# A pipelined six-layer local-attention kernel: the layer loop written out as 96 steps, and four changes to the order on TensorE and ScalarE

## The reference, cut to what matters

```python
def attn_layer(x, Wqkv, qs, ksc, Wo):       # 16 heads of 64, windows of 32 tokens
    q, k, v = split(x @ Wqkv)               # 128 -> 3 * 1024
    q = rotary(l2norm(q) * qs); k = rotary(l2norm(k) * ksc)
    out = local_attention(q, k, v)          # each window looks at itself and the one before
    return out @ Wo                         # 1024 -> 128

def ffn_layer(x, g, bln, W1, b1, W2, b2):
    a, gate = split((layernorm(x) * g + bln) @ W1 + b1)   # 128 -> 2 * 341
    return a * gelu(gate) @ W2 + b2                      # 341 -> 128

for i in range(6):
    x = attn_layer(shift_tokens(x), Wqkv[i], ...) + x
    x = ffn_layer(shift_tokens(x), ...) + x
```

## Time and profile before

| | |
|---|---|
| runs, us | 4669.51, 4648.67, 4651.01; median 4651.01 |
| the profiled execution | 4670.98 us, its span 4669.2 us |
| busy: PE, its weight loads, DVE, ACT, POOL | 89%, 59%, 62%, 56%, 60% |
| mean granted TensorE clock | 0.959 of full speed |
| DMA engines | mean 55 GB/s, 258.77 MB |

### The profile page before, as it was taken

How to read it: one execution, slowest core, us unless ns; L and a number is a source line. 1 busy time by engine, 2 the same in 40 slices (tenths; PEclk the granted TensorE clock), 3 DMA queues, 4 the chain that set the end, 5 groups by cost and what they waited for, 6 DMA issues and landing times. The chain is left out here.

```text
span 4669.2 us, 162098 instructions
## 1 busy us (share of the span) xinstructions
PE 4135.5 (89%) x67078; PEld 2766.5 (59%) x67078; DVE 2915.5 (62%) x4217; ACT 2616.0 (56%) x4417; POOL 2805.6 (60%) x3584
## 2 busy tenths in 40 slices
PE   5879788689999999999999999999999999999994
PEld 2434344346666666666666666666666666666663
DVE  5565656466666666666666666666666666666664
ACT  2545353446666656656656566566665656656552
POOL 0000000177777777777777777777777777777771
PEclk8989798889999999999999999999999999999997
DMA  0000000112222222222222223222222222222223
GB/s 28 3 15 2 15 2 15 41 39 65 65 70 74 58 68 67 72 55 67 66 70 64 56 68 79 62 59 70 68 72 55 65 66 70 64 56 67 70 64 81
DMA packets 284568, 258.77 MB, mean 55 GB/s; under 512 B 122871, under 2 KB 258508, under 8 KB 271148
## 3 DMA queue, kind: packets, MB, share of 16 engines
q1 hardware_dynamic: 283820, 248.14, 20.0%
HBM read 117.63 MB, written 29.77 MB: 32 GB/s over the span
## 5 line engine op out<-in xcount | busy, mean ns | idle before, releaser
L787 DVE TENSOR_TENSOR products<-bank_d,table 128x1024 f32<-128x1024 f32 x772 | 938.1, 1216 | 684.4 <-ACT sq L614 679.7
L910 POOL TENSOR_TENSOR products<-products 128x2048 f32<-128x2048 f32 x192 | 871.0, 4536 | 313.8 <-DVE products L787 313.8
L413 PE MATMUL bank_d<-w_qkv,xT 128*128 128x512 f32 x1544 | 807.5, 626 | 18.7 <-issue 13.0
L614 ACT ACTIVATE sq<-bank_d 128x512 f32<-128x512 f32 x772 | 468.0, 606 | 469.9 <-PE bank_d L413 457.4
L947 POOL TENSOR_TENSOR qk_rot<-products,rnorm 128x2048 f32<-128x2048 f32 x192 | 695.6, 3623 | 14.0 <-POOL rnorm L929 12.7
L785 DVE TENSOR_REDUCE ss<-sq 128x16 f32<-128x1024 f32 x386 | 468.8, 1214 | 229.3 <-ACT sq L614 229.3
L874 POOL MEMSET ident<- 128x128 f32 x1 | 0.2, 205 | 915.1 <-POOLq L1064 915.1
L954 POOL TENSOR_TENSOR prob<-prob,inv_sum 128x1024 f32<-128x1024 f32 x192 | 365.4, 1903 | 307.3 <-DVE inv_sum L767 307.3
L1491 DVE TENSOR_REDUCE part_max<-s_max 128x1 f32<-128x512 f32 (+3 forms) x768 | 399.5, 554 | 152.2 <-PE s_max L1240 101.3
L478 PE MATMUL scores<-kT,qT 64*32 64x64 f32 x24576 | 430.4, 218 | 24.4 <-issue 24.4
L413 PE MATMUL bank_a<-w_qkv,xT 128*128 128x512 f32 x768 | 403.1, 607 | 49.7 <-ACT gate L669 47.5
(11 more groups left out here) (168 smaller groups left out, 7581.9 us busy)
## 6 DMA issues: line engine op xcount, KB each, us to landing
v_back<-v SPq DMA_DIRECT2D x96, 768.0 KB, 5.4
w_qkv<-in_Wqkv_dram SPq DMA_DIRECT2D x25, 1024.0 KB, 5.1
v_back<-v SPq DMA_DIRECT2D x192, 128.0 KB, 5.7
w_qkv<-in_Wqkv_dram SPq DMA_DIRECT2D x25, 512.0 KB, 5.4
xs<-x_layers SPq DMA_DIRECT2D x194, 64.0 KB, 2.1
w_o<-in_Wo_dram SPq DMA_DIRECT2D x24, 512.0 KB, 6.9
xr<-x_layers SPq DMA_DIRECT2D x96, 128.0 KB, 3.0
x<-x SPq DMA_DIRECT2D x96, 128.0 KB, 1.8
```

Of the source, the lines that this page charges most:

```text
L413: nc.tensor.matmul(bank[:, :], xT[:, P * a:P * (a + 1)], w_qkv[:, col:col + 512], start=True, stop=True).then_inc(d_filled if i < 8 else a ...
L614: nc.scalar.activation(sq[j % 2][:, 8 * c:8 * c + 8, :], bank_d[slot][:, :].rearrange("p (h d) -> p h d", d=DH), ACT.Square).then_inc(squa ...
L787: nc.vector.tensor_tensor(products[:, a, head:head + 8, :, :].rearrange("p h r (o d) -> p h r o d", o=2), bank[:, :].rearrange("p (h r d) ...
L910: link(nc.gpsimd.tensor_tensor(products[:, a, :, 0, :], products[:, a, :, 0, :], products[:, a, :, 1, :], ALU.add))
```

## The change

It does seven things, all in `local_layers`.

1. `rounds` writes out all 96 steps; `Step` now carries the layer and the sequence as plain numbers, so that every address and semaphore value is a constant.
2. The weights, the rows for the rotary table and the table itself are loaded or made once for each layer.
3. `QK_ORDER`: the tile a = 1 is transposed and copied as q half 0, k half 0, q half 1, k half 1, and each half of the scores waits for its own half of k alone.
4. ACT copies `yT` before the exponentials of phase 1; before, it did so after them.
5. PE fills `aB` (FFN up) directly after `aA`, before projection 9.
6. PE does the FFN down part right before the products with v, and ACT copies `y2T` right after `xT`; in the ring `y2T` moves ahead of the four `O` names, which gives all five another bank.
7. The matmul of two columns ahead of each `times_v` is gone.

The diff, cut to its core (the other places follow from the new `Step`):

```diff
+QK_ORDER = (0, 1, 2, 3, 4, 6, 5, 7)
...
-        ring_a = Ring([(f"qk{i}", 1) for i in range(8)]
+        ring_a = Ring([(f"qk{i}", 1) for i in QK_ORDER]
                       + [v0, ("xn", 3), ("yT", 2), ("gA", 3), ("PT0", 1), ("PT1", 1), v1, ("gB", 3), v2,
-                         ("PT2", 1), ("PT3", 1), v3, ("xT", -1)]
-                      + [("O00", 1), ("O01", 1), ("O10", 1), ("O11", 1), ("y2T", 3)])
+                         ("PT2", 1), ("PT3", 1), v3, ("xT", -1), ("y2T", 3)]
+                      + [("O00", 1), ("O01", 1), ("O10", 1), ("O11", 1)])
...
-            for b in range(BATCH):
-                for p in range(POS):
-                    step_fn(Step(b, p))
-            with nc.Fori(1, DEPTH, engines=[eng.engine], hint_back_edge=True) as layer:
+            for layer in range(DEPTH):
                 for b in range(BATCH):
                     for p in range(POS):
-                        step_fn(Step(BATCH * layer + b, p))
+                        step_fn(Step(layer, b, p))
...
-                if runs(now) and s.p == POS - 1:
+                if runs(now) and s.b == BATCH - 1 and s.p == POS - 1:
                     sp.wait_ge(d_filled, chunk_at(now, 7)[1] + 1)
-                    load_w_qkv(s.f + 1, 0, 2 * INNER, wqk_in)
+                    load_w_qkv((s.layer + 1) % DEPTH, 0, 2 * INNER, wqk_in)
...
-                if runs(back2) and s.p == 1 and in_rounds(s):
+                if runs(back2) and s.b == 0 and s.p == 1 and in_rounds(s):
 
-                    load_wo(s.f)
+                    load_wo(s.layer)
...
                 banks = [fill_a(s, f"O{half}{u}", after="PT3") for u in range(2)]
-
-                nc.tensor.matmul(banks[1][:, 0:2], ident_b[:, :], ident_b[:, 0:2], start=True, stop=True)
...
             def score(s, pair, ph, half):
+                pe.wait_ge(a_free, ring_a.at(s, f"qk{6 + half}")[1] + 1)
                 if half == 0:
-                    pe.wait_ge(a_free, ring_a.at(s, "qk7")[1] + 1)
...
                     if runs(back1):
-                        transpose_qk(s, back1, 2 * i)
-                        transpose_qk(s, back1, 2 * i + 1)
+                        transpose_qk(s, back1, QK_ORDER[2 * i])
+                        transpose_qk(s, back1, QK_ORDER[2 * i + 1])
...
                 if runs(back3):
                     ffn_up(s, "aA")
+                    ffn_up(s, "aB")
                 project_now(9)
                 if runs(back3):
                     ffn_up(s, "gB")
-                    ffn_up(s, "aB")
                 project_now(10)
...
                     transpose_x(s)
+                if runs(back3):
+                    ffn_down(s)
                 if runs(back1):
                     times_v(s, back1, 0)
                 project_next(0)
...
                     times_v(s, back1, 1)
                 project_next(2)
-                if runs(back3):
-                    ffn_down(s)
                 project_next(3)
...
-                if runs(back1):
-                    exponentials(back1, 1)
                 if runs(back2):
                     bank = filled(s, "yT")
                     nc.scalar.activation(yT[:, :], bank[:, 0:PAIR], ACT.Copy).then_inc(a_free, 1)
+                if runs(back1):
+                    exponentials(back1, 1)
...
                 if new.exists:
                     copy_x(s)
+                if runs(back3):
+                    bank = filled(s, "y2T")
+                    nc.scalar.activation(y2T[:, :], bank[:, 0:PAIR], ACT.Identity,
+                                         bias=small[:, SMALL["b2"]:SMALL["b2"] + 1]).then_inc(a_free, 1)
...
-                    make_table(s.f + 1, s.p)
+                    if s.b == BATCH - 1:
+                        make_table(s.layer + 1, s.p)
```

More of the change, by code:

```diff
@@ L55, in names_of_step @@
     def names_of_step(self, t):
-        return [n for n, _ in self.stage_names] if isinstance(t, int) and MAX_LAG <= t < PAIRS else self.names(t)
+        return self.names(t)
     def last_in_bank(self, step, name):
@@ L119, in __init__ @@
         self.f = step.f + q // POS
+        self.layer = step.layer + (step.b + q // POS) // BATCH
         self.n = step.t - lag
@@ L559, in step @@
                 if runs(back3):
-                    if s.p == 3:
-                        pe.wait_ge(wffn_in, 64 * (s.f + 1))
+                    if s.b == 0 and s.p == 3:
+                        pe.wait_ge(wffn_in, 64 * (s.layer + 1))
                     ffn_up(s, "gA")
@@ L718, in step @@
                 square(new, 2)
-                if runs(back3):
-                    bank = filled(s, "y2T")
-                    nc.scalar.activation(y2T[:, :], bank[:, 0:PAIR], ACT.Identity,
-                                         bias=small[:, SMALL["b2"]:SMALL["b2"] + 1]).then_inc(a_free, 1)
                 square(new, 3)
             act.wait_ge(constants_ready, INIT)
-            copy_x(Step(-1, POS - 1))
+            copy_x(Step(-1, BATCH - 1, POS - 1))
             for i in range(EARLY):
-                square(Step(-1, POS - 1).pair(-1), i)
+                square(Step(-1, BATCH - 1, POS - 1).pair(-1), i)
             rounds(act, step)
@@ L829, in step @@
                 if runs(back3):
-                    if s.p == 3:
-                        dve.wait_ge(wffn_in, 64 * (s.f + 1))
+                    if s.b == 0 and s.p == 3:
+                        dve.wait_ge(wffn_in, 64 * (s.layer + 1))
                     hidden_units(s, "A")
```

81 lines of the change are left out of this document (41 added, 40 removed).

## The result

The changed kernel takes 4632.86 us (median of 20 runs, 4612.02 to 4656.98); the kernel before took 4662.38 beside it (20 runs). The ratio is 0.9945, 95% interval 0.993 to 0.996: 0.55% faster, just over what can be told from no change, where 3.2% was forecast. 4500 was predicted, with 4425 to 4575 as the range; the time lies above it. The profiled execution of the changed kernel took 4644.36 us, span 4642.6, mean granted clock 0.950 (before: 4670.98, 4669.2, 0.959).

The account below looks back on a forecast made before the run. PE, busy 89% of the span, was taken as the bound, with stops for instruction packets on top. Reordering saves 161 us over 92 steps, layer 0 loses 10: 4651 - 151 = 4500 us, range 4425 to 4575.

Parts of the forecast that it names:

- the loop's excess of 1.24: Irregular time per loop step above the steady 36.72 us, from PE's instruction stops; assumed to stay on all 92 steps.
- The order: Reordered work on PE and ACT: steady step from 36.72 to 34.97 us, 1.75 less, 161 us over 92 steps.
- FFN down: Moved before the products with v, it covers PE's wait for ACT's copies: 0.63 us a step, plus 0.10.
- POOL's chain to xn: DVE finishes the early projections' last product some 0.35 us later and POOL follows: 0.04 us a step taken off.
- the 0.10 of late start behind projection 2: FFN down no longer starts late in its old place: 0.10 us a step gained.
- `yT` with the half heads: Copying `yT` before phase 1's exponentials lets projection 9 start 0.31 us earlier; q and k by halves gain nothing by themselves.
- The matmuls of two columns: Two in a step ahead of the products with v, partly overlapped; removing them gains 0.22 us, between 0 and 0.36.
- The weights at zero: Loading weights and tables once for each layer gains nothing, since no row of PE waits for either.
- A: Rival: instruction stops vanish with the loop, 265 us less, 4386 us; chance 0.08.
- C: Rival: instruction fetching becomes the bound, a stop with its clock costs 4.5 us, 186 us more, 4837 us; chance 0.04.
- B: Rival: waits around `yT` and the gates only change place; 0.95 a step remains, 77 us less, 4574 us; chance 0.15.
- D: Rival: the order gives nothing since DVE sets the step; within 10 us of 4651; chance 0.03.

Follow-up runs that it names:

- phase_bad_late: The changed kernel with ten satisfied waits a step on PE, and `v_back` issued only after the second half of the products with v; 4435.81 us.
- phase_bad: The changed kernel with ten satisfied waits a step on PE, holding the boundary behind the issue of `v_back`; 4740.92 us.
- late_after: The changed kernel with one more wait on SP, so `v_back` is issued only after the second half of the products with v; 4457.65 us.
- new_order_loop: The kernel before, with its loop and weight loads, and only parts 3 to 6 of the change; 4746.21 us.
- after_reload: The changed kernel with the weights loaded again for each sequence, tables still once in a layer; 4690.68 us.
- phase_good: The changed kernel with ten satisfied waits a step on PE and 160 once at step 3, putting the boundary before the issue of `v_back`; 4445.15 us.
- best_late: The changed kernel with late `v_back`, ten satisfied waits a step ahead of the transposes of q and k, and phase 1's exponentials before the `yT` copy; 4433.60 us.

## Why the prediction was wrong

**The step that failed** is "So I put the loop's excess of 1.24 on all 92 steps". Measured 2.47, which is 92 x 1.23 = 113 us, most of the distance from the forecast to the result (133); the smaller gain of the order is another 92 x 0.27 = 25. The paragraph had what was needed: the stops stand in straight code, a packet is about 250 instructions, and the boundaries wander through the products with v. What it lacked was the other half, what makes a boundary harmful. I named packets queued behind `v_back` as a possibility and used it only to say that fewer weights would help little. Had I gone through the steps of the trace before and set the boundary against SP's issue of `v_back`, two things would have come out: that the bad zone lies behind that issue, and that the change widens it. The copy of v and with it `v_back` kept their place while FFN down moved in front of the products: `v_back` was issued 1.01 us after PE had begun them (2534.17 against 2533.16) and is now issued at 0.06 (first row SP, second PE, both of the changed kernel):

```profile
2164.76 0.54 SPq L358 DMA_DIRECT2D v_back<-v  x1
```
```profile
2164.70 0.32 PE L440 MATMUL bank_a<-probT,v_back 64*64 64x32 f32 x8
```

The first half of the products is 256 instructions in 2.00 us, so these 0.95 us are worth about 120 of them. In the loop of the kernel before, whose boundaries lay at sixteen fixed places of the first half, stops were seen at the 231st and 241st instruction and, from the boundary one packet on, at the 6th and 16th. In its written-out layer 0 the boundary lay at about the 155th to 161st, also behind the issue, and 3 of 13 steps stopped, so such a place is not harmful every time. In the changed kernel the slow steps, but for two, are those with the boundary at the 108th to 255th and at the 1st to 20th, about two thirds of all places, and a drift of five a step goes through all of them.

**The order**, forecast 1.75 and measured 1.48, was right in kind and place. `aB`: 0.43, exact. FFN down: 0.46 instead of 0.73; I had taken off 0.04 for POOL's chain to xn, and it was 0.18, and the 0.10 of late start behind projection 2 did not appear. `yT` with the half heads: 0.32, where 0.31 was forecast for `yT` and nothing for the half heads. Alone they give 0.27 and 0.47, so the sum held by luck and the causal sentence didn't hold. The matmuls of two columns: forecast 0.22, not priced by a run of their own.

**The weights at zero** was wrong in the changed kernel (58 us) and right in a kernel with good boundaries (-2 us). The condition I should have named was "no boundary falls behind a load".

**The rivals.** A (the stops go with the loop) fell: written out, the old order lost some 130 us. Its rule is that of the Trainium skill, "Runtime: NRT & Kernel Launch", section on instruction fetch mechanics: blocks of 256 instructions (the trace agrees, 16.4 KB a packet), each crossing mostly hidden. The traces agree where no large transfer is ahead (phase_bad_late, 0.11 us a step over the clean one) and not where a megabyte is (phase_bad, 3.28). C had the price and the place nearly right: its point of balance was 51 slow steps of 92 at 4.5 us; there were 62, at 3.7 each (227 / 62). It had a chance of 0.04, and its cause, density alone, was the wrong one. B and D fell: 35.23 is a clean step under both. Of the signs set out in advance, an excess over 2.5 was to mean C, and it came to 2.47, just short; 10 to 25 stops were to show the forecast right, and there were 73 of over 0.9 us.

**Still open.** Why some packets come late while the engines are nearly idle, as in late_after. What the loop costs by itself: new_order_loop and after_reload differ by 56 us, but their boundaries lie differently too. The loop with a late `v_back` was not tried. Nor was it tried to issue `v_back` in smaller pieces, or from another queue.

## What to carry to other kernels

Stops with "issue" as their reason amid dense small matmuls were here instruction packets that came late; look up which DMA was issued ahead of the boundary, one packet of instructions before each stop (6.5 us before the stop shown), and move that DMA, before believing any gain of 3% or less from a reordering. Any edit that changes the number of instructions on the bounding engine also shifts every boundary after it: eighty idle instructions were worth 296 us here, so compare two orders by their clean step as well as by their time. Here a large transfer did least harm where no boundary fell behind it, or where PE was busy with long matmuls; if it can't go there, pad the period to whole packets and choose the offset.

## What the runs showed of the hardware that was not expected

- An instruction packet got no precedence over data: ahead of 49 of the changed kernel's 73 pauses, with the 16 DMA engines at least 85% busy, it began 2.2 to 5.9 us after the boundary; over all boundaries the median is 1.1 us. Some packets were late without that (4.41 us in late_after, with the engines 1.4% busy before it).
- A late packet costs twice: the stop (1.3 us in the step shown) and then a stretch at 0.50 of the clock. That step was 38.35 - 35.23 = 3.1 us over the clean one.
- Ten satisfied waits, five instructions, cost a step 0.09 us (phase_good) and 0.30 (best_late, part of it through the wait for `yT` behind them) ahead of the transposes of q and k, and nothing ahead of the second scores, where PE is idle.
- One wait added on SP made the kernel 3.8% faster (4632.86 to 4457.65).
